# Graph attention and expert layer on one core: one-hot matrices made in two stretches of levels instead of four

## The reference, cut to what matters

```python
e = leaky_relu(a_s[src] + a_d[dst], 0.2)
m = segment_max(e, dst); p = exp(e - m[dst]); s = segment_sum(p, dst)
out = segment_sum(xw[src] * (p / s[dst])[:, :, None], dst)
```

## Time and profile before

| what | value |
|---|---|
| median of three runs | 3036.93 us |
| profiled execution | 3038.06 us |
| its span, first to last instruction | 3036.2 us |
| mean granted TensorE clock over the span | 0.835 |
| VectorE busy | 2092.3 us (69%) |
| TensorE, weight loads busy | 2009.3 us (66%) |
| GpSimd busy | 1891.8 us (62%) |
| ScalarE busy | 1786.1 us (59%) |

### The profile page before, as it was taken

One profiled execution on the slowest core, in us unless ns is written; L12 is line 12 of the kernel. 1 busy time (PEld: TensorE's weight loads), 2 busy tenths in 40 slices (PEclk: granted clock), 3 DMA queues, 4 the chain that ended last, 5 costly groups with the idle time before them and its releaser, 6 DMA issues.

```text
span 3036.2 us, 42924 instructions
## 1 busy us (share of the span) xinstructions
PE 2122.6 (70%) x11674; PEld 2009.3 (66%) x11675; DVE 2092.3 (69%) x4422; ACT 1786.1 (59%) x2613; POOL 1891.8 (62%) x1868
## 2 busy tenths in 40 slices
PE   4600003778887888888878888603449999999998
PEld 2400003778887788787878787603438999999997
DVE  7678867777777777777777777788864444444443
ACT  5424424888888888888888888624433333333332
POOL 5777777777777777777777777777771222222222
PEclk8855556889998999898999898855559999999999
DMA  9446994444444444444444444555772222222222
GB/s 356 135 145 180 159 239 122 127 127 158 132 127 127 143 147 127 128 158 131 128 127 158 133 127 128 170 206 174 260 258 37 37 38 37 38 38 37 38 37 31
DMA packets 278910, 395.04 MB, mean 130 GB/s; under 512 B 156236, under 2 KB 231569, under 8 KB 272257
## 3 DMA queue, kind: packets, MB, share of 16 engines
q1 hardware_dynamic: 202945, 244.92, 25.8%
q0 software_dynamic: 74000, 145.58, 21.6%
q10 hardware_dynamic: 1840, 3.06, 0.3%
HBM read 201.61 MB, written 191.79 MB: 130 GB/s over the span
## 4 chain that ended last, share of the span: by engine, by line
POOL 47%; PE 25%; issue 16%; DVE 5%; DMA 2%; DVEq 1%; ACT 1%; SPq 1%; POOLq 0%; ACTq 0%
POOL AR L932 43%; PE ps L1440 12%; PE ps L1446 12%; POOL adstart L894 1%; POOL placed L999 1%; DMA tables<-AR 1%; POOL room L971 1%; DVE group_stats L1987 1%; ACT AR L1258 1%; DVE AR L1705 1%; SPq L379 0%; SPq L609 0%; DVE AR L2111 0%; DVE AR L2108 0%; DVE AR L2047 0%
## 5 line engine op out<-in xcount | busy, mean ns | idle before, releaser
L932 POOL DMA_INDIRECT AR<-tables,idx x1391 | 1329.8, 956 | 425.8 <-issue 423.5
L1354 PE MATMUL ps<-table_parts,onehot 128*128 128x408 f32 (+1 forms) x5848 | 1194.2, 369 | 304.5 <-ACT onehot L1214 213.3
L1354 PEld LDWEIGHTS ps<-table_parts,onehot 128*128 128x128 f32 x5848 | 1160.0, 208 | 338.7 <-DVE AR L1817 185.3
L1139 ACT COPY AR<-AR 128x1984 f32<-128x1984 f32 (+3 forms) x110 | 402.6, 3660 | 255.4 <-DVE AR L1752 212.6
L1008 POOL DMA_INDIRECT out<-AR,idb x105 | 185.0, 1762 | 567.6 <-issue 536.6
L1752 DVE TENSOR_TENSOR_SCAN AR<-ps,AR 128x512 f32<-128x512 f32 x404 | 454.2, 1197 | 0.0
L1440 PEld LDWEIGHTS ps<-AR 128*128 128x128 f32 x3360 | 393.2, 193 | 31.8 <-issue 26.5
L1440 PE MATMUL ps<-AR 128*128 128x128 f32 x3360 | 393.8, 276 | 26.4 <-DVE AR L2205 26.4
L1745 DVE TENSOR_TENSOR AR<-AR,ps 128x3968 f32<-128x3968 f32 (+1 forms) x51 | 357.5, 7010 | 5.8 <-ACT AR L1158 5.8
L1214 ACT ACTIVATE onehot<-onehot 128x2048 fp32r<-128x2048 f32 (+1 forms) x172 | 347.6, 2021 | 5.5
L2205 DVE COPY AR<-AR 128x1024 f32 x210 | 151.6, 722 | 207.2 <-PE ps L1440 205.7
(11 more groups left out here) (342 smaller groups left out, 2345.5 us busy)
## 6 DMA issues: line engine op xcount, KB each, us to landing
state<-AR SPq DMA_DIRECT2D x50, 2232.0 KB, 9.5
AR<-tables,idx POOLq DMA_INDIRECT x1440
AR<-in_L_ffn_W SPq DMA_DIRECT2D x16, 1024.0 KB, 9.7
AR<-placed SPq DMA_DIRECT2D x420, 32.0 KB
AR<-adstart SPq DMA_DIRECT2D x50, 248.0 KB, 4.0
adstart<-room SPq DMA_DIRECT2D x21, 496.0 KB, 13.5
tables<-AR SPq DMA_DIRECT2D x49, 136.0 KB
room<-tables SPq DMA_DIRECT2D x14, 476.0 KB, 4.4
```

Source lines behind the costliest of these rows:

```text
L932: pool.indirect_dma_start(out=G[s][:, j, 0:ROWT], out_offset=None, in_=table_rows, in_offset=bass.IndirectOffsetOnAxis(ap=idx[:, s, j:j + ...
L1139: return S.copy(to.rearrange("p j (h c) -> p j h c", h=HD)[:, :, :, a:z], of[:, :, 1:n + 1].rearrange("p (c h) j -> p j h c", h=HD)[:, :, ...
L1354: return T.matmul(bank[:, 0:z], mark, table_parts[:, k, v * w:v * w + z], start=(a == 0 and k == 0), stop=(a == LEV - 1 and k == PARTS - 1))
```

## The change

The levels are divided in two stretches, of 9 and 8 levels. The same 17 `Abs` and the same elements of `Relu` are written per batch, in two `Relu` instructions instead of four. Stretch 0 of batch b+2 is marked after the whole copy of batch b; nothing is marked between the halves of the copy any more. Stretch 1 of batch b+1 is marked after the decays of batch b, where stretches 2 and 3 were. All counts of semaphores are worked out from the number of stretches, so TensorE's, VectorE's, SyncE's and GpSimd's waits follow without an edit.

```diff
-STRETCHES = ((0, 5), (5, 9), (9, 13), (13, 17))
+STRETCHES = ((0, 9), (9, 17))
...
                 if by_pe(b + 1):
-                    mark_stretch(b + 1, 2)
-                    mark_stretch(b + 1, 3)
+                    mark_stretch(b + 1, 1)
...
                     copy_channels(G[s][:, 0:n, 0:F], TS[:, 0:F, :], n, half * CH // 2, (half + 1) * CH // 2)
-                    if half == 0 and by_pe(b + 2) and b + 2 > PE0:
-                        mark_stretch(b + 2, 0)
                 S.copy(G[s][:, 0:n, F:ROWS], TS[:, F:ROWS, 1:n + 1].rearrange("p f j -> p j f")).then_inc(rows_copied, 1)
...
                 if b == PE0 - 1:
                     mark_stretch(b + 1, 0)
-                    mark_stretch(b + 1, 1)
...
                 copy_back(b, w)
                 if by_pe(b + 2) and b + 2 > PE0:
-                    mark_stretch(b + 2, 1)
+                    mark_stretch(b + 2, 0)
```

## The result

The changed kernel takes 3050.9 us (median of 5 runs, 3049.96 to 3051.6) against 3036.93 for the kernel before (5 runs, 3034.85 to 3039.28): a ratio of 1.0042, 95% interval 1.0029 to 1.0055. It is slower by 14 us; forecast were 18. Its profiled execution took 3051.15, with a span of 3049.4.

What follows compares the result with a forecast made beforehand. GpSimd's gathers bound the kernel at 33.88 us a batch; the two-batch chain, 35.5 + 27.8 + 5.7 = 69.0, 34.5 each, puts batch 49 24.8 late; less 4.3, taken as 18 slower: 3055 us, range 3038 to 3067.

Steps and rivals of the forecast that it cites:

- The bound and its cover: GpSimd's 27 gathers per batch set the pace, 33.8 us; VectorE's wait for them, about 5.5 us, is the only cover.
- The chain up to TensorE's start: From batch start through scans, copy (end 25.6 us) and nine levels marked, TensorE starts at 35.5 us.
- ScalarE's slack: ScalarE's copies and marks end 35.5 us after batch start, next weights are due at 36.7: slack shrinks to 1.2 us.
- Columns and marks: VectorE takes TensorE's columns and does the marks behind them: 5.5 us, with 0.2 of handovers 5.7.
- the 136 products: TensorE's matmuls for one batch in one run: 25.7 us plus 2.1 for the clock's loss, 27.8.
- the prediction's own sign: If TensorE's 136 products take other than 27 to 28.5 us, the sum's second half is wrong.
- rival A: Not slower: gathers stay the bound, TensorE's products take 26.6 us, clock loss 0.9; 3037, within 3035 to 3042; chance 0.14.
- What is given back: Behind the last batch, VectorE's 4.30 us wait for one row (L1925) absorbs lag; GpSimd forgives 7, the smaller counts.
- B: Much slower: TensorE's clock stays low for longer, loss 3.4 us, 35.15 a batch, +46 us, 3083; chance 0.04.
- C: ScalarE becomes the bound: its weights slip, a handover 1 us longer in each batch, 20 us more, 3075; chance 0.04.
- D: Faster: batches wait for ScalarE, larger operations relieve it, two Relu of 0.2 us in 43 batches, 3020; chance 0.03.

Runs made afterwards that it cites:

- two runs with 26 gathers: GpSimd fetches 26 columns instead of 27 per batch: in the kernel before 2983.6 us (0.9821), in the changed kernel 3051.1 us (1.0046).
- the run with the copy's rows last: Changed kernel with its first stretch marked ahead of the copy's last 1.1 us (rows of scores and maxima): 3037.7 us, 1.0001.
- order only: Kernel before with its four stretches, but stretch 0 of batch b+2 marked behind the whole copy of batch b: 3037.6 us, 0.9997.
- last two merged: Kernel before with only its last two stretches merged, giving 5, 4 and 8 levels: 3037.0 us, 0.9994.
- nine between halves: Changed kernel with its first stretch of 9 levels marked between the halves of the copy: 3038.8 us, 1.0002.
- the run with eight levels: Changed kernel with stretches of 8 and 9 levels instead of 9 and 8: 3039.5 us, 1.0007.

## Why the prediction was right, and where its numbers were off

**The bound and its cover: right.** Gathers set the pace, 33.8 us a batch, and the cover was VectorE's wait of 5.5 us for them. The two runs with 26 gathers show the first; the vanished wait shows the second.

**The chain up to TensorE's start: right in every second batch.** 25.6 for the copy's end was 25.9, 35.5 for TensorE's start was 35.7 (1275.05 to 1310.73). In the batches behind a short distance they were 26.6 and 36.35. The prediction said of ScalarE's slack that it "shrinks to 1.2 us, and is not gone"; that holds for batches evenly spaced. At a distance of 31.4 us the copies and marks still end 35.5 after the batch's start, but the next weights are due at 31.4 + 2.9 = 34.3. Columns and marks: 5.7 was 5.5.

**The term that was mis-sized is TensorE's.** I took 27.8 us for the 136 products, 2.1 of it for the clock. They took 26.8 in the mean (1153.8 us over 43 batches): in the rows above 27.1 behind the long stops and 26.4 behind the short, so the loss over the 25.7 at full clock is 0.7 to 1.4. By the prediction's own sign, 27 to 28.5 us, this term failed, if narrowly. With the rows' values the sum is 35.7 + 27.1 + 5.5 = 68.3 from the batch at 1275.05 to the next but one, and 36.35 + 26.4 + 5.5 = 68.3 from the one at 1306.42: twice the 34.15 measured, in both chains. The granted clock behind a stop of 4.9 us and one of 9.8 (us, busy per engine, granted clock, DMA share, GB/s):

```profile
1274.46:1278.46 4.00, 4.00 (x17) 3.92 (x18) 3.56 (x10) 0.56 (x2) 3.09 (x4) 0.59 0.34 95
1278.46:1300.91 22.45, 22.45 (x121) 22.08 (x120) 17.96 (x13) 18.54 (x16) 16.96 (x19) 1.00 0.24 56
1310.73:1314.73 4.00, 4.00 (x14) 3.92 (x15) 3.52 (x1) 4.00 (x9) 3.09 (x4) 0.50 0.36 105
1314.73:1337.80 23.07, 23.06 (x124) 22.69 (x123) 13.62 (x11) 19.57 (x16) 17.52 (x19) 0.99 0.35 89
```

The stops of 9.8 us cost only 0.6 us more than those of 4.9, and the latter no more than the stop of 3.79 of before (26.59). I had read three rows of 64 products behind stops of 6.4 to 8.2 us as the price of a long stop. In all three another stop, between batches, had come one piece of work before. That alone doesn't explain them: in the run with the copy's rows last TensorE also stops once a batch, and behind stops of 6.15 and 6.25 us the same products took 26.30 and 27.80, a loss of 0.6 and of 2.1. So 2.1 does occur behind one stop, the length of a stop doesn't tell its price, and what else decides it isn't shown.

The products of the changed kernel take less time in sum because the engine stops less often: 40 stops in the 40 batches from 616 to 1971 us, all over 4 us, where before had 61 of 1 us or more. It is the later place that joins the products and not the larger stretches: order only, with four stretches, also has 40 stops, and last two merged and nine between halves have 64 and 72 of 1 us or more. The pages' rows for the products, first the kernel before, then the changed one (busy us and mean ns, then idle time):

```profile
L1354 PE MATMUL ps<-table_parts,onehot 128*128 128x408 f32 (+1 forms) x5848 | 1194.2, 369 | 304.5 <-ACT onehot L1214 213.3
```

```profile
L1350 PE MATMUL ps<-table_parts,onehot 128*128 128x408 f32 (+1 forms) x5848 | 1153.8, 362 | 373.9 <-ACT onehot L1211 373.9
```

40 us less work in 43 batches, 0.9 us a batch. The advice that I had set against my own reading, the Trainium skill's in "TensorE: Matmul & The Clock Gate" (section "HAM oscillation — how this bites in real kernels"), to do the work contiguously before the next wait, holds in this measure. It wasn't enough for rival A. With the other terms as measured, A needed products of 67.8 - 35.7 - 5.5 = 26.6 us in one chain and 25.9 in the other; they took 27.1 and 26.4, so A failed by 0.5 us in two batches. How near A was is shown by the run with eight levels.

**The start of the stage was missed.** The period gives 40 x (34.15 - 33.88) = 10.8 us of the 17.7 by which batch 49 starts later (1989.2 against 1971.6). The other 6.9 were there at batch 9 (623.3 against 616.4). The profiles of kernels that mark behind the whole copy have batch 9 at 621.8 to 628.9 (order only 623.4), those that mark earlier at 616.4 to 619.7. Some 3 of the 6.9 look like luck of the profiled execution of before: its batch 5, ahead of any code that differs, started at 472.2, the other profiles from 473.6 to 477.5; the three runs that fetch 27 columns and mark earlier have batch 9 at 619.2 to 619.7. The rest goes with the later place. Where gathers set the pace this is caught up: order only started batch 49 at 1975.1, near the 1971.6 of before. In the changed kernel nothing catches up. I didn't look for this in the trace of before, and the runs don't settle its cause.

**What is given back: right.** The 17.7 us late at batch 49 became 13.4 at L1921 (2038.88 against 2025.50 in the earlier trace rows), 4.3 less, which is VectorE's former wait for its row; the span is 13.2 longer. GpSimd's wait for TensorE before its first L971 was 1.2 us and cost nothing. So the mechanism was right, but that the 18 of the forecast lies so near the 14 measured is in part luck, since its errors cancel. Over 40 batches, which are 20 of two each, it had 20 us too much for the products and 4 for the columns, and 10 too little for the time up to TensorE's start; 7 were missed at the start of the stage, and 2.5 I had rounded off downwards.

**The rivals.** A failed by 0.3 us a batch. B is out: every second stop was near 9.8 us, and no products in the changed kernel lost more than 2.0 behind a stop, where B wanted 3.4. C is there in part: in every second batch ScalarE's weights were late, and VectorE waited 10.8 us for them in 19 waits, where C had 1 us in each batch. D, that ScalarE is relieved by larger operations, is out: the last two merged gains nothing.

## What to carry to other kernels

An engine's wait for the bound engine is a budget that every chain behind it shares: write out each chain from one batch's start to a later batch's start, divide by the batches that it spans, and compare with the pace, before pieces are merged or moved. Here two harmless edits (larger stretches, a later place) were harmful together, and the split of 9 and 8 stood 0.35 us a batch on the wrong side of an edge (34.15 against the 33.8 of the runs that lose nothing). Check each engine's slack for the shortest distance between batches and not for the mean. Putting 1.1 us of unurgent copy behind the urgent marks took the whole loss away again, though no version that does the full work beat the kernel before, as its gathers set the pace.

## What the runs showed of the hardware that wasn't expected

- TensorE: in the changed kernel the loss hardly grows with the stop: 136 products took 26.44 us behind 4.98 us of idleness and 27.07 behind 9.81. In each the engine runs at 1.2 GHz for a time (granted clock 0.50 over the first 2 us) and then at 2.4 GHz. The number of stops counts for more than their sum: 1194.2 us of products with 61 stops of 1 us or more and 304.5 us of idleness before, 1153.8 with 40 stops and 373.9 us after.
- But stops of like length can cost differently: 26.59 us behind 3.79 and 28.09 behind 4.38 in the kernel before (at 1693.59 and 1319.85), 26.30 behind 6.15 and 27.80 behind 6.25 with the copy's rows last. A few rows don't give the price of a stop; the mean over the stage does.
- Two interleaved chains kept an uneven distance (near 36.9 and 31.4 us in turn) over the whole stage. The terms show what can hold it: one chain has the long stop and products 0.6 us longer, the other waits 0.6 us for ScalarE, so both take 68.3 us. That this is the reason is argued and not tested.
- Left open: whether the changed kernel would be as fast as before with TensorE at 2.4 GHz throughout. An estimate from the terms above says yes: 36.0 (the mean of the two chains' 35.7 and 36.35) + 25.7 + 5.5 = 67.2 us, 33.6 a batch, under the gathers' 33.8. No run keeps the clock up during the stops.
